# Three graph layers on one core: where the dense products of the chunk in front stand in TensorE's order

## The reference

```python
# layer 0: relational, with a residual and a layer norm
msg = (x[src] + rel_emb[type]) @ W_msg.T + b_msg
x1  = layernorm(x + x @ W_self.T + b_self + segment_mean(msg, dst))
# layer 1: SAGE with swish
h = segment_mean(x1[src], dst) @ W1_l.T + b1 + x1 @ W1_r.T
h = h * sigmoid(h)
# layer 2: SAGE, with a residual over both and a layer norm
out = layernorm(x1 + segment_mean(h[src], dst) @ W2_l.T + b2 + h @ W2_r.T)
```

## Time and profile before

| | |
|---|---|
| median of 3 runs | 366.36 us (366.32 to 366.43) |
| the profiled execution | 366.51 us |
| its span | 364.7 us |
| mean granted TensorE clock | 0.994 of full speed |
| PE busy | 335.0 us (92% of the span), 3385 matmuls |
| DVE busy | 232.8 us (64%), 597 instructions |
| ACT busy | 173.9 us (48%), 385 instructions |

### The profile page before, as it was taken

One profiled execution on the slowest core, in us unless ns is written; L12 is line 12 of the kernel. 1 busy time (PEld: TensorE's weight loads), 2 busy tenths in 40 slices (PEclk: granted clock), 3 DMA queues, 4 the chain that ended last, 5 costly groups with the idle time before them and its releaser, 6 DMA issues.

```text
span 364.7 us, 9187 instructions
## 1 busy us (share of the span) xinstructions
PE 335.0 (92%) x3385; PEld 250.4 (69%) x3385; DVE 232.8 (64%) x597; ACT 173.9 (48%) x385; POOL 4.9 (1%) x17
## 2 busy tenths in 40 slices
PE   0689999999999999999999999999999999999970
PEld 0579998998998998998984454555474455455460
DVE  6999988998999999999446942330345031431454
ACT  1585667769778878778522141331252131121040
POOL 5000000000000000000000000000000000000000
PEclk9999999999999999999999999999999999999997
DMA  4700000000000000000000000000000001100102
GB/s 138 171 2 4 2 2 3 4 2 4 2 2 2 3 4 3 3 2 2 24 16 3 0 0 2 0 2 0 0 2 3 0 1 31 29 2 29 30 2 67
DMA packets 8523, 5.38 MB, mean 15 GB/s; under 512 B 370, under 2 KB 8476, under 8 KB 8476
## 3 DMA queue, kind: packets, MB, share of 16 engines
q1 hardware_dynamic: 8188, 4.32, 4.4%
q10 hardware_dynamic: 288, 0.43, 0.3%
HBM read 3.14 MB, written 1.60 MB: 13 GB/s over the span
## 4 chain that ended last, share of the span: by engine, by line
PE 84%; DVE 8%; ACT 4%; issue 2%; DMA 1%; ACTq 0%; DVEq 0%
PE ps L943 54%; PE ps L891 16%; PE ps L1009 5%; PE ps L1019 3%; PE ps L962 2%; ACT counts L834 2%; DVE hot L1182 1%; PE ps L989 1%; DMA counts<-dst_t 1%; PE ps L898 1%; PE ps L908 1%; DVE hot L1175 1%; DVE table L1192 1%; ACT new_first L812 1%; ACT scaled L790 1%
## 5 line engine op out<-in xcount | busy, mean ns | idle before, releaser
L943 PE MATMUL ps<-counts,table 128*128 128x256 f16 (+2 forms) x1350 | 214.6, 309 | 0.0
L943 PEld LDWEIGHTS ps<-counts,table 128*128 128x128 f16 x1350 | 114.9, 97 | 74.2 <-issue 0.2
L834 ACT CAST counts<-ps 128x494 f32 x208 | 107.7, 578 | 45.5 <-PE ps L891 44.9
L891 PE MATMUL ps<-hot 128*128 128x156 f16 (+1 forms) x584 | 67.9, 241 | 15.6 <-DVE hot L1182 15.0
L891 PEld LDWEIGHTS ps<-hot 128*128 128x128 f16 x584 | 53.1, 103 | 17.3 <-DVE hot L1182 15.3
L1182 DVE TENSOR_TENSOR hot<-iota,edges 128x1200 f16<-128x1200 f16 x73 | 56.6, 775 | 0.0
L1175 DVE TENSOR_TENSOR hot<-iota,edge_rows 128x768 f16<-128x768 f16 x73 | 40.1, 550 | 4.9 <-PE ps L928 4.6
L898 PE MATMUL ps<-window_hot,hot 128*128 128x19 f16 x292 | 42.5, 181 | 0.0
L1272 DVE TENSOR_TENSOR new_first<-ps,scaled 128x512 f32<-128x512 f32 (+1 forms) x9 | 5.4, 600 | 54.0 <-ACT scaled L790 54.0
L1272 DVE TENSOR_TENSOR hot<-ps,scaled 128x512 f32<-128x512 f32 (+1 forms) x8 | 5.1, 639 | 41.6 <-ACT scaled L790 41.6
L898 PEld LDWEIGHTS ps<-window_hot,hot 128*128 128x128 f16 x292 | 28.9, 99 | 0.7
(11 more groups left out here) (135 smaller groups left out, 320.3 us busy)
## 6 DMA issues: line engine op xcount, KB each, us to landing
table<-x SPq DMA_DIRECT2D x2, 768.0 KB, 5.1
out<-new_first SPq DMA_DIRECT2D x3, 256.0 KB
out<-hot SPq DMA_DIRECT2D x3, 256.0 KB, 2.4
counts<-first_dst ACTq DMA_DIRECT2D x1, 208.0 KB, 3.9
counts<-dst_t SPq DMA_DIRECT2D x1, 208.0 KB, 4.5
counts<-type_t ACTq DMA_DIRECT2D x1, 208.0 KB, 4.7
counts<-src_t SPq DMA_DIRECT2D x1, 208.0 KB, 5.0
hot<-w_l SPq DMA_DIRECT2D x2, 64.0 KB, 2.0
```

Source lines behind the costliest of these rows:

```text
L834: nc.scalar.copy(A[:, HALVES[half], bass.ds(bases[group % 8], GROUP_W)], window(group, half)).then_inc(copied[half], 1)
L891: return nc.tensor.matmul(window(group, half)[:, :, at[t]], row(tiles[t], LOW_AT, P), blocks_of(tiles[t], half), start=group == half == t ...
L943: last = nc.tensor.matmul(ps[:, sums_bank(q), first:first + width], table[:, b, part, :], A[:, b, at:at + width], start=b == part == 0, st ...
```

## The change

In TensorE's order the layers 1 and 2 had `dense(q-1)` behind `aggregate(q)` and `turn(q)`, apart from the first chunk of a layer, where it stood behind 8 of the 25 source blocks. Now it stands behind 4 source blocks (`SUB` = 4) for every other full chunk as well, q = 8 to 12 and 15 to 19. The first chunk of a layer keeps its 8, the last one, of 53 nodes, its old order. ScalarE's order follows: in these chunks `lead(q)` and `turn_out(q)` come after `scale`, `gate` or `root`, and `high` of q-1. VectorE's and SyncE's programs are as they were, and so are all semaphores.

```diff
             for q in range(EARLY, ALL_CHUNKS):
-                opens = chunk_of(q) == 0
-                if not opens:
+
+                ahead = CHUNKS <= q and tiles_of(q) > 1
+                if not ahead:
                     lead(q)
                 if q > EARLY:
                     scale(q - 1)
-                if not opens:
+                if not ahead:
                     turn_out(q)
                 if layer_of(q - 1) == 1:
                     gate(q - 1)
@@
                     high(q - 1)
-                if opens:
+                if ahead:
                     lead(q)
                     turn_out(q)
@@
             for q in range(CHUNKS, ALL_CHUNKS):
-                if chunk_of(q) == 0:
-                    aggregate(q, range(0, 2 * SUB))
+                if tiles_of(q) > 1:
+                    cut = 2 * SUB if chunk_of(q) == 0 else SUB
+                    aggregate(q, range(0, cut))
                     dense(q - 1, all_tiles(q - 1))
-                    aggregate(q, range(2 * SUB, BLOCKS))
+                    aggregate(q, range(cut, BLOCKS))
                     turn(q)
                 else:
                     aggregate(q, range(BLOCKS))
```

## The result

| | median, us | runs | lowest to highest |
|---|---|---|---|
| kernel before, beside it | 365.40 | 12 | 364.51 to 367.43 |
| changed kernel | 363.41 | 12 | 361.75 to 364.73 |

The ratio is 0.9929 with a 95% interval of 0.9906 to 0.9952. The forecast, 363.6 against 366.36, is a ratio of 0.9925.

A forecast was written before the change was run, and what follows sets the result against it. The prediction took TensorE's stream of matmuls, plus what hangs behind its last product, to bound the kernel. Its terms, -0.60 - 1.64 - 0.55 = -2.79 us on a median of 366.36, gave 363.6 us, range 363.1 to 364.5.

The forecast's parts named there:

- The stall before dense(12): Between the last two layers, dense(12) held by preset(12): the wait goes altogether, -0.60 us.
- The tail: From dense(18) to the kernel's end: dense(19), scale(19) and add_up(19) come sooner, -1.64 us.
- The seams: Ten moved dense products: first pass's weight load hides behind an aggregation matmul, 0.055 us each, -0.55 us.
- The 0.03 added to scale(19): In the tail, scale(19) 1.14 us behind dense(19) plus 0.03 for the first pass after a very short matmul.
- How the numbers follow: Last step: range 363.1 to 364.5; 0.73 us counted as measurable; faster 0.90, same 0.05, slower 0.05.
- The sum is put on the median: Step from terms to time: -2.79 us applied to the runs' median of 366.36, giving 363.6 us.
- lead(8): ScalarE's copy at q = 8, behind high(7): late by 0.1 us at most, against 0.78 of slack.
- the 0.78 forecast: Slack in us between the end of ScalarE's two copies of chunk q-1 and the moved dense(q-1).
- The drain: Rival: every dense inside an aggregation drains the array, +0.18 us for each of ten; 365.9 us, chance 0.05.
- Seams without gain: Rival: the seams give nothing, only the layer boundary and tail pay; 364.1 us, chance 0.09.
- All waits vanish: Rival: TensorE's three waits of 0.44, 1.18 and 1.98 us all go, plus the seams; 362.2 us, chance 0.03.
- ScalarE's row work holding up the copies: Slower rival: copies of chunk q wait for q-1's row work, costing above 11.7 us; 370.6 us, chance 0.05.

The follow-up runs named there:

- layer 1 alone: Against the kernel before, the move made only for q = 8 to 12; 365.27 us, ratio 0.9965, 0.88 us less in the trace from turn(7) on.
- the seams alone: Against the kernel before, the move made only for q = 8 to 11 and 15 to 18; 364.85 us, ratio 0.9971.
- the runs with 64 and 96 columns: Changed kernel with the ten moved dense products cut to the first 64 or 96 nodes of each tile; trace from turn(7) on 157.11 and 154.60 us.
- one and two blocks in front: Changed kernel with moved dense products behind one or two source blocks instead of four; 367.77 us (one run) and 365.02 us (one run).
- TensorE's order alone: Changed kernel's TensorE order with ScalarE's order as in the kernel before; 381.47 us, one run.

## Why the prediction was right, and which step of it failed

**Terms.** Sum and mechanism held in the traces. The stall before dense(12): 0.60 forecast; 0.60 is what layer 1 alone gave beyond five seams. The tail: 1.64, and 1.65 in the same way. The seams: 0.55, measured 0.056 each, 0.56 for ten. The sum 2.79, measured 2.79 in the stretch, and one remaining wait of 1.7 as forecast. The 0.03 added to scale(19) had no row behind it; in the changed kernel scale(19) stands 1.17 behind dense(19), the 1.14 and the 0.03 (350.37 to 351.54).

**The step that failed.** It is the last one, from the sum to what a measurement would say ("How the numbers follow"): "0.2% of 366.4 is 0.73 us, about what a measurement of this kernel can tell from no change", with 0.90 put on faster and 0.05 on the same. That step took three runs, 0.11 us apart, for the spread of this kernel. Twelve runs of each kernel spread over 2.9 and 3.0 us, and the interval of the ratio reaches 0.23% to each side. That tells a gain of 0.7% from nothing, but fixes its size only to a third of itself; and by a margin of 2%, where this prediction took 0.2%, the outcome is "the same", to which it had given 0.05.

**In part luck.** "The sum is put on the median" failed with it. The 366.36 was a middle group's time, and with twelve runs the median of the kernel before was 365.40. Less 2.79 that would be 362.6, 0.8 below the 363.41 measured. That 363.6 lies so near rests on the changed kernel's median falling into its middle group too, where it has 6 of 12 executions.

**What settles the size.** By medians the kernel gained 1.99 us, by the ratio 2.6, by the stretch 2.79. The first two depend on how many executions fall into which group. Group against group (medians 364.56, 366.34 and 367.41 before, 361.81, 363.46 and 364.69 after) the gain is 2.8, 2.9 and 2.7, which agrees with the stretch; the groups were made after the times were seen. The run of the seams alone shows the trap: its ratio of 0.9971 would be 1.1 us, over twice its 0.45 in the stretch, with 6 of its 12 executions in the shortest group and 2 of the 23 of the kernel before beside it.

**Moved at no cost.** No TensorE wait for a copy appeared, and lead(8) wasn't late. But the 0.80 of slack found and the 0.78 forecast agree by luck: I counted 1.20 for the two copies, whose rows overlap, and which took 1.08 (216.21 to 217.29), and nothing for the 0.10 from the copy's end to TensorE. For lead(8) I had up to 0.1 of lateness, as a bound that kept the whole of the rows' 3.77 from add_up(7) to the end of high(7); it was 2.75 (212.58 to 215.33), as the table load of 1.28 ran while ScalarE waited for the checks.

**The drain.** The nearest row by place, q = 14, said +0.24 a dense, the nearest by shape said nothing. Choosing by shape was right, and the runs with 64 and 96 columns show why. Had I gone by place, the forecast would have been 365.9.

**Rivals.** Seams without gain: refuted by their own run. All waits vanish: refuted, the 1.67 stayed. ScalarE's row work holding up the copies: not so in the changed kernel, and no run made that work longer, so the bound of 11.7 us is untested. The run without ScalarE's half shows another cost of its order, 16.4 us.

## What to carry to other kernels

When a product of chunk q-1 is ready before chunk q's long stream ends, place it a little way inside that stream, far enough that the copies it needs are over; then move the engine that takes its result in the same edit, or the gain turns into a loss. Look for the gain at the ends: in the steady middle the stream had no hole, and what was won there were seams of 0.056 us. A wait that ends last on TensorE is not yet time: ask whether the waiting product or the work beside it sets the end. Here 1.2 us of a wait of 1.7 went, and what was won was the 0.4 that VectorE's chain had lost. And when a kernel's times fall into groups, compare group with group, or a stretch of the trace behind the part that varies.

## What the runs showed of the hardware

**A waiting matmul pays beyond its wait.** A float32 dense that has to wait for ScalarE starts 0.10 us behind the copy and takes 0.08 more over its first products (1.13 for 1.05); its first weight load then starts 0.03 ahead of the first pass, where it is 0.22 ahead otherwise. With one and two blocks in front the kernel lost 0.55 and 0.12 us a dense in all.

**A float32 dense between matmuls of 128 columns pays 0.21 to 0.25 us more with a stationary of 64 columns, and nothing more with 96.** Against 96 columns, 0.15 of it lies in the first products and 0.10 in the aggregation matmuls behind the dense.

**The counting part has several lengths.** The start of the stretch lies at 201.5 to 201.7 in four of the twelve profiled executions, at 203.1 to 203.4 in seven and at 204.5 in one, and no edit touches the counting part. From group to group these starts are about 1.7 and 1.2 us apart, the times of the kernel before 1.8 and 1.1. From 20 to 30 us (busy time, counts, then TensorE's granted clock) the run of the seams alone shows

```profile
20.00:30.00 10.00, 8.43 (x103) 7.73 (x104) 10.00 (x20) 7.43 (x15) 0.00 (x0) 0.83 0.01 3
```

and the kernel before

```profile
20.00:30.00 10.00, 8.83 (x95) 8.50 (x93) 9.21 (x19) 6.21 (x12) 0.00 (x0) 1.00 0.01 3
```

In the first, 201.5 at the end, VectorE (third column) has no hole and the granted clock is 0.83; in the second, 203.3 at the end, VectorE has holes at a clock of 1.00. All four traces with the short counting part look like the first (10.00 of VectorE, 0.83); the seven at 203.1 to 203.4 have 8.9 to 9.3 of VectorE, at clocks from 0.50 to 1.00 and the same end. So a lower clock there doesn't decide it by itself; what does stays open, and no run was made for it. The one at 204.5, TensorE's order alone, looks like the kernel before in these 10 us, but its granted clock is 0.61 from 168 to 170 us and 0.53 from 170 to 172, where the other traces have 1.00 from 160 to 186; that fits its extra 1.1 us, and isn't tested.
